# The cosine attention of a two-layer megakernel, written out straight in batches of six tiles instead of a loop over heads in batches of four

## Chip, core and metric

One core of one Trainium2 chip. The metric is device time in microseconds (us) of one launch, median of several runs.

## What is computed

X is (2, 2048, 256) in float32. Each of two layers forms `x + attention(LN(x)) * silu(ffn(LN(x)))` with 16 heads of 16 columns. Layer 0 has an inverse-distance attention and stays as it was. Layer 1, which the change rewrites:

```
Q, K = l2norm(heads(x Wq)), l2norm(heads(x Wk)); V = heads(x Wv)
cos = clip(Q K^T, -0.999, 0.999)
W = (1 - arccos(cos) / pi) ** 16;  W = W / (sum(W) + 1e-6)
out = (W V) Wo + bo
ffn = relu(x Wq1^T + b1) Wq2^T + b2        (Wq1, Wq2 ternary)
```

## The kernel before

`program` runs phases one after the other, each a block of five engine programs: weights, norm, projection, attention, output, for each layer. `attention_phase` serves both layers by `if L == 0`.

A **unit** is 128 keys of one head and one batch entry against all 2048 queries: 128 x 2048 float32, 32 units a head, 512 in layer 1. For each unit of layer 1: TensorE forms the scores in two PSUM halves `psS` (L751); VectorE clips each half into a slot of `ring` (L1054) and multiplies it with itself from PSUM into `q_ring` (L1063); ScalarE takes Ln(1 - cos^2) (L1011) and Sigmoid of -0.5 times that (L1016); VectorE multiplies with the cosine, the tangent of half the angle ("tangents", L1094); ScalarE takes Arctan (L1021). The 16th power is then split by columns: ScalarE does 1312 of 2048 by Ln and Exp (L1027, L1033), VectorE 224 by one affine instruction and four squarings (L1074, L1078), GpSimd (POOL) 512 in the same way (L712, L716). TensorE then adds the weighted values into `psO` (L774).

The work goes in **batches** of `BATCH = 4` units, eight a head; `ring` has eight slots (two batches) and `q_ring` four. ScalarE's instructions take two units at a time except Sigmoid (one). A `powers` call on VectorE or POOL handles a batch as two halves, each one affine and four squarings, taken alternately, so ten instructions. ScalarE changes its table set twice a batch: before Sigmoid and before the second Ln.

Order on each engine for batch j: VectorE: clip and square of batch j, powers of j-1, tangents of j. ScalarE: Ln, Sigmoid, Arctan, table load, Ln, Exp, of j. POOL: powers of j, after **both** Arctans of the batch (`pool.wait_ge(s_at, ...)`, L707). TensorE: scores one unit ahead, then the weighted values of j-1. In every fourth batch comes the work of a **tile** n (16 units, one head and batch entry): ScalarE copies the head's output (L820), TensorE transposes it (L782), VectorE divides it by its sum (`dve_out`, L838 to L855) into `gated` in SBUF, and 128 tokens of the FFN pass: hidden (L795, L801), Relu (L827), sum (L810), copy (L833), and a store issued from ScalarE (L835). Hidden stands in one piece behind the weighted values of its batch.

`pairs` (L668) gives TensorE, ScalarE, VectorE and SyncE the first head, a `Fori` loop over 14 heads, and the last head; POOL's program is straight. SyncE loads the stacks of the next tile (12 DMAs) and `ffn_in`. POOL copies each head's values into `v_tile` (L704). The output phase of layer 1 finds `gated` in SBUF and loads two arrays in four pieces each (`n_loads`, L1124); that of layer 0 loads three.

Of the kernel before, what the change touches and what calls it, by code (L numbers as in the profile page):

```python
# [52 lines left out]
class Mem:  # L53


    def __init__(self, nc, ctx):
# [351 lines left out]
def projection_phase(nc, m, io, L):  # L408
# [23 lines left out]
    with ExitStack() as ctx:  # L432
# [6 lines left out]
        (s_xT,) = sems(nc, ctx, pre, "xT_stored")  # L439
# [3 lines left out]
        def _(sp):  # L443
# [21 lines left out]
            if L == 1:  # L465
                sp.wait_ge(s_xT, 16)
            if L == 0:
# [166 lines left out]
def attention_phase(nc, m, io, L):  # L634


    pre = f"a{L}"
# [3 lines left out]
    q_ring = m.area(RING * T, 4, T)  # L641
# [3 lines left out]
    ACT_POW, DVE_POW = 1312, 1536  # L645
    POW_STEPS = 10
    BATCH = 4
    ACT_SQ = 384
    rows = ROWS + NORM_ROWS if L == 0 else ROWS
    loads = 2 * len(PRODUCTS) + (2 if L == 0 else 0)  # L650
    values = m.values[:, :, :].rearrange("p (b k) (h d) -> p b k h d", b=B, h=HEADS)
    gated = m.gated[:, :, :].rearrange("p (b q a) (h d) -> p b q a h d", b=B, q=QB, h=HEADS)
    EPS_SUM = SHEP_EPS if L == 0 else SUM_EPS1
    with ExitStack() as ctx:
# [3 lines left out]
        if L == 0:  # L658
            s_a, s_y, s_m, s_v, s_wa, s_wd, s_r2, s_g0 = sems(
                nc, ctx, pre, "inv_dist", "quot", "guarded", "inv_shifted", "w_act", "w_dve", "ffn_squared", "gated0")  # L660
        else:
            s_cl, s_q, s_rs, s_ls, s_z, s_at, s_ln, s_w, s_pw, s_pp = sems(
                nc, ctx, pre, "clipped", "cos2", "rsin", "log_sin", "tan_half", "angle", "log", "w_act", "w_dve",
                "w_pool")
# [11 lines left out]
        def _(sp):  # L676
            def head(h, first, last):
                for b in range(B):
# [4 lines left out]
                    for side, stack in ((0, m.q_stack[b]), (1, m.k_stack[b])):  # L683
# [4 lines left out]
                        if L == 0:  # L688
                            at = ROWS + 3 * side
                            sp.dma_start(stack[at:at + 3, :],  # L690
                                         io["norm_parts"][:, bass.ds(h + HEADS * side, 1), tok]
                                         .rearrange("a o t -> (a o) t")).then_inc(s_stk[b], 16)
# [7 lines left out]
        def _(pool):  # L700
            def value_tile(h, b, first):
                if not first:
# [3 lines left out]
            def powers(h, j):  # L706
                pool.wait_ge(s_at, UNITS // 2 * h + 2 * j + 2)  # L707
                at = (BATCH * j) % RING
                parts = [ring[:, at + 2 * i:at + 2 * i + 2, DVE_POW:T] for i in range(2)]
                done = POW_STEPS * (UNITS // BATCH * h + j)  # L710
                for part in parts:
                    nc.gpsimd.tensor_scalar(part, part, 2.0 / PI, 0.5, ALU.mult, ALU.add).then_inc(s_pp, 1)  # L712
                for i in range(2, POW_STEPS):
                    part = parts[i % 2]
                    pool.wait_ge(s_pp, done + i - 1)
                    nc.gpsimd.tensor_tensor(part, part, part, ALU.mult).then_inc(s_pp, 1)  # L716

            def guard(c):
                pool.wait_ge(s_y, 2 * c + 2)
                if c + 1 >= LAG_SQ:  # L720
                    pool.wait_ge(s_wd, c + 2 - LAG_SQ)
# [3 lines left out]
            def head(h, first, last):  # L725
                if L == 0:
                    for u in range(UNITS):
                        if u % KT == 3:
                            value_tile(h, u // KT, first)
                        guard(UNITS * h + u)  # L730
                else:
                    for j in range(UNITS // BATCH):
                        if j == 0:
                            value_tile(h, 0, first)
                        if j == 2:
                            value_tile(h, 1, first)
                        powers(h, j)
            for h in range(HEADS):
                head(h, h == 0, h == HEADS - 1)

        def pe_scores(pe, h, u, first, halves=(0, 1)):
# [3 lines left out]
            for half in halves:  # L745
                if not (first and u == 0):

                    pe.wait_ge(s_y if L == 0 else s_q, 2 * (UNITS * h + u) + half - 1)
# [7 lines left out]
        def pe_values(pe, h, u, first):  # L756
# [8 lines left out]
            if L == 0:  # L765
                pe.wait_ge(s_wa, n + 1)
                pe.wait_ge(s_wd, n + 1)
            else:
                pe.wait_ge(s_w, n + 1)
                pe.wait_ge(s_pw, POW_STEPS * (UNITS // BATCH * h + u // BATCH + 1))  # L770
                pe.wait_ge(s_pp, POW_STEPS * (UNITS // BATCH * h + u // BATCH + 1))

# [13 lines left out]
        def pe_hidden(pe, n, quarters=range(4)):  # L786

            for quarter in quarters:
# [3 lines left out]
                for f in range(2 * (quarter % 2), 2 * (quarter % 2) + 2):  # L792
                    for k in range(KD):
                        c = (4 * g + f) * P
                        last = nc.tensor.matmul(m.psM[g][:, f * P:(f + 1) * P], m.w1T[:, k, c:c + P],  # L795
                                                m.ffn_in[:, k, :], start=k == 0 and (L == 0 or f == 0),
                                                stop=L == 0 and k == KD - 1)
                if quarter % 2 == 0:
                    continue
                if L == 1:  # L800
                    last = nc.tensor.matmul(m.psM[g][:, :], m.b1_tiles[:, :],  # L801
                                            m.ident[0:FT, 4 * g:4 * g + 4].unsqueeze(2).broadcast_to([FT, 4, P]),
                                            start=False, stop=True)
                last.then_inc(s_h, 1)

        def pe_ffn_sum(pe, n, fs=range(FT)):
            if fs[0] == 0:
                pe.wait_ge(s_r if L == 1 else s_r2, 2 * (n + 1))
            for f in fs:
                last = nc.tensor.matmul(m.psM[0][:, 0:D], m.hidden[:, f, :], m.w2T[:, f, :], start=f == 0,  # L810
                                        stop=L == 0 and f == FT - 1)
            if L == 1:
                last = nc.tensor.matmul(m.psM[0][:, 0:D], m.ones_row[0:1, :], m.b2_row[0:1, :], start=False, stop=True)
# [24 lines left out]
        def dve_out(dve, h, b, n):  # L838
# [5 lines left out]
            nc.vector.tensor_scalar(den, ps[:, :, :, DH], EPS_SUM, None, ALU.add).then_inc(s_den, 1)  # L844
# [5 lines left out]
            if L == 0:  # L850
                nc.vector.tensor_tensor(out, ps[:, :, :, 0:DH], out, ALU.mult).then_inc(s_g0, 1)
                dve.wait_ge(s_g0, n + 1)
                nc.vector.tensor_tensor(out, out, rec16, ALU.mult).then_inc(s_g, 1)
            else:
                nc.vector.tensor_tensor(out, ps[:, :, :, 0:DH], rec16, ALU.mult).then_inc(s_g, 1)  # L855

        if L == 0:

            OUT_COPY, OUT_T, OUT_DIV = 5, 7, 8
            HID = (0, 1, 2, 3)  # L860
            RELU, SQ = (2, 4), (4, 6)
            SUM = {8: (0,), 9: (1,), 10: (2,), 11: (3,), 12: (4,), 13: (5,), 14: (6, 7)}
            COPY = 15

            @block.tensor
            def _(pe):
                def head(h, first, last):
                    for u in range(UNITS + (LAG_PV if last else 0)):
                        b, kt = u // KT, u % KT
                        n = 2 * h + b  # L870
# [408 lines left out]
```

## Time and profile before

| | us |
|---|---|
| median of 3 runs | 7410.69 (7410.47 to 7413.83) |
| the profiled execution | 7411.12 |
| its span in the trace | 7409.3 |
| layer 1, first to last start of a batch's tangents | 2843.81 to 7290.03 |

Busy time of each engine over the span: VectorE 6974.3, ScalarE 6691.4, TensorE 4119.9, POOL 3180.5. Read a row as: start, length, engine, line, operation, output<-input, shape, count; in brackets the idle time before it and what ended it.

### The profile page before, as it was taken

What the parts mean: (1) busy time and instruction counts of PE and PEld (TensorE: products, weight loads), DVE (VectorE), ACT (ScalarE), POOL (GpSimd) and SP (SyncE); (2) the same over time, 40 slices, a digit from 0 to 9 for tenths busy, and PEclk for the clock granted to TensorE, in tenths of its full rate; (3) what the DMA queues carried; (4) which work ended last, traced back from release to release, by engine and by line L of the source; (5) the groups of instructions that cost most, each with busy time, mean ns of one, the idle gap of its engine ahead of it and who ended that gap; (6) DMA issues with size and microseconds to landing.
All of it is one profiled execution on the core that took longest, in us unless ns stands there. A gap on an engine that the chain in (4) does not pass through costs nothing. (4 is left out here: it accounts for less than half of the span.)

```text
span 7409.3 us, 61195 instructions
## 1 busy us (share of the span) xinstructions
PE 4119.9 (56%) x17232; PEld 1274.3 (17%) x17232; DVE 6974.3 (94%) x6415; ACT 6691.4 (90%) x4385; POOL 3180.5 (43%) x1860
## 2 busy tenths in 40 slices
PE   6666666676666774444445444444444444444445
PEld 3222222222222331111111111111111111111112
DVE  7899999999999768999999999999999999999996
ACT  3799999999999647999999999999999999999995
POOL 0244444444444203544554454454445445544542
PEclk8888888888888886556566656656666666666657
DMA  3100000000000221000000000000000000000002
GB/s 129 46 18 17 12 17 12 17 17 12 17 14 15 100 84 32 7 6 11 7 6 11 7 6 11 7 6 11 7 6 7 10 6 7 11 6 7 11 2 70
DMA packets 113682, 148.47 MB, mean 20 GB/s; under 512 B 17038, under 2 KB 98857, under 8 KB 112634
## 3 DMA queue, kind: packets, MB, share of 16 engines
q1 hardware_dynamic: 104314, 138.54, 6.1%
q10 hardware_dynamic: 9216, 8.39, 0.3%
q14 instruction: 116, 0.95, 0.0%
q8 instruction: 36, 0.59, 0.0%
HBM read 91.55 MB, written 55.31 MB: 20 GB/s over the span
## 5 line engine op out<-in xcount | busy, mean ns | idle before, releaser
L751 PE MATMUL psS<-q_stack,k_stack 102*128 102x512 bf16 (+1 forms) x4096 | 1756.3, 523 | 2397.0 <-DVE work L1063 1619.6
L716 POOL TENSOR_TENSOR work<-work 128x1024 f32<-128x1024 f32 x1024 | 1915.9, 1907 | 10.2
L774 PE MATMUL psO<-work,v_tile 128*32 128x512 f32 x8192 | 1378.6, 794 | 729.8 <-DVE work L1078 722.8
L723 POOL TENSOR_SCALAR work<-work 128x2048 f32<-128x2048 f32 x512 | 970.5, 1896 | 1527.0 <-DVE work L955 1274.8
L1054 DVE TENSOR_SCALAR work<-psS 128x1024 f32<-128x1024 f32 x1024 | 1207.3, 1220 | 74.9 <-issue 41.0
L943 DVE SCALAR_TENSOR_TENSOR work<-work,psS 128x1024 f32<-128x1024 f32 x1024 | 1216.1, 1216 | 51.3 <-ACT work L901 50.2
L712 POOL TENSOR_SCALAR work<-work 128x1024 f32<-128x1024 f32 x256 | 267.5, 1045 | 2305.1 <-ACT work L1021 2294.9
L1063 DVE TENSOR_TENSOR work<-psS,work 128x1024 f32<-128x1024 f32 x1024 | 1201.5, 1216 | 0.0
L1094 DVE SCALAR_TENSOR_TENSOR work<-work 128x2048 f32<-128x2048 f32 x512 | 1138.9, 2287 | 62.3 <-ACT work L1016 60.5
L901 ACT ACTIVATE work<-psS 128x1024 f32<-128x1024 f32 x1024 | 1062.2, 1038 | 119.0 <-PE psS L751 86.0
L1011 ACT ACTIVATE work<-work 128x4096 f32<-128x4096 f32 x256 | 922.7, 3612 | 130.4 <-DVE work L1063 120.4
L916 ACT ACTIVATE work<-work 128x2048 f32<-128x2048 f32 x512 | 986.4, 1927 | 2.6 <-POOL work L723 2.2
L955 DVE TENSOR_TENSOR work<-work 128x1664 f32<-128x1664 f32 x512 | 970.1, 1895 | 0.2 <-ACT work L916 0.2
L751 PEld LDWEIGHTS psS<-q_stack,k_stack 102*128 102x128 bf16 (+1 forms) x4096 | 269.6, 106 | 3995.6 <-DVE work L1063 2520.0
L1016 ACT ACTIVATE work<-work 128x2048 f32<-128x2048 f32 x512 | 935.9, 1898 | 1.4
L1021 ACT ACTIVATE work<-work 128x4096 f32<-128x4096 f32 x256 | 924.1, 3610 | 6.9
L1027 ACT ACTIVATE work<-work 128x2624 f32<-128x2624 f32 x256 | 597.9, 2383 | 1.4
L1033 ACT ACTIVATE work<-work 128x2624 f32<-128x2624 f32 x256 | 595.7, 2374 | 0.0
L1078 DVE TENSOR_TENSOR work<-work 128x448 f32<-128x448 f32 x1024 | 572.4, 629 | 0.0
L774 PEld LDWEIGHTS psO<-work,v_tile 128*32 128x32 f32 x8192 | 250.3, 135 | 1560.7 <-issue 808.3
L1074 DVE TENSOR_SCALAR work<-work 128x448 f32<-128x448 f32 x256 | 293.7, 1187 | 3.8 <-ACT work L1021 3.8
L795 PEld LDWEIGHTS psM<-ffn_in,w1T 128*128 128x128 f32 x2048 | 270.9, 202 | 75.3 <-issue 57.9
(126 smaller groups left out, 3186.7 us busy)
## 6 DMA issues: line engine op xcount, KB each, us to landing
qk_parts<-work SPq DMA_DIRECT2D x64, 384.0 KB, 3.2
q_stack<-qk_parts SPq DMA_DIRECT2D x384, 64.0 KB, 2.2
k_stack<-qk_parts SPq DMA_DIRECT2D x384, 64.0 KB, 2.2
ffn_in<-xT_store SPq DMA_DIRECT2D x64, 128.0 KB, 2.5
y_store<-ffn_out ACTq DMA_DIRECT2D x64, 128.0 KB, 1.7
work<-y_store SPq DMA_DIRECT2D x8, 1024.0 KB, 12.0
work<-in_x SPq DMA_DIRECT2D x1, 4096.0 KB, 14.4
xn_store<-work SPq DMA_DIRECT2D x1, 4096.0 KB, 13.0
```

Of the source, the lines that this page charges most:

```text
L716: nc.gpsimd.tensor_tensor(part, part, part, ALU.mult).then_inc(s_pp, 1)
L723: nc.gpsimd.tensor_scalar(slot, slot, F32_MAX, 0.0, ALU.min, ALU.max).then_inc(s_m, 1)
L751: last = nc.tensor.matmul(m.psS[half][:, q * 512:(q + 1) * 512], m.k_stack[b][0:rows, kt * P:(kt + 1) * P], m.q_stack[b][0:rows, c:c + 512 ...
L774: last = nc.tensor.matmul(m.psO[b][VW * q:VW * (q + 1), :], m.v_tile[b][:, kt, :], ring[:, u % RING, q * 512:(q + 1) * 512], start=kt == 0 ...
L901: nc.scalar.activation(ring[:, u % RING, half * 1024:(half + 1) * 1024], m.psS[half][:, :], ACT.Abs_reciprocal_sqrt, bias=ZERO_SHIFT)\
L916: nc.scalar.activation(slot, slot, ACT.Abs_reciprocal_sqrt, bias=SHEP_EPS * SHEP_EPS, scale=2 * SHEP_EPS).then_inc(s_v, 1)
L943: nc.vector.scalar_tensor_tensor(part, part, 0.5 / SHEP_EPS, m.psS[half][:, :], ALU.add, ALU.mult).then_inc(s_y, 1)
L955: nc.vector.tensor_tensor(part, part, part, ALU.mult).then_inc(s_wd, 1)
L1016: nc.scalar.activation(slot, slot, ACT.Sigmoid, scale=-0.5).then_inc(s_rs, 1)
L1054: nc.vector.tensor_scalar(ring[:, u % RING, half * 1024:(half + 1) * 1024], m.psS[half][:, :], COS_MAX, -COS_MAX, ALU.min, ALU.max)\
L1063: nc.vector.tensor_tensor(q_ring[:, u % BATCH, cols], m.psS[half][:, :], ring[:, u % RING, cols], ALU.mult).then_inc(s_q, 1)
L1094: nc.vector.scalar_tensor_tensor(slot, q_ring[:, u % BATCH, :], RSIN_MAX, slot, ALU.min, ALU.mult).then_inc(s_z, 1)
```

## The change

Layer 0's attention becomes `distance_phase`, instruction for instruction as before. Layer 1's becomes `cosine_phase`:

- no loop on any engine: 86 batches written out, sizes 4, 84 times 6, 4;
- one region of 18 slots: two batches of cosines (12) and one of squares (6). `values` and `gated` lie in it, so the projection phase stores the values to DRAM (`v_store`), SyncE loads each tile's values from there straight into `v_tile` (rows of 64 bytes), and each head's output goes from a small staging buffer to `o_store`, also by SyncE; the output phase loads it back (three loads a piece) and its transposes wait for that;
- first Ln in instructions of 3, 2 and 1 units, Sigmoid of 1, 1, 2, 2, Arctan, the later Ln and Exp of 3 and 3;
- column split 1328 / 192 / 528 (ScalarE / VectorE / POOL) instead of 1312 / 224 / 512;
- POOL's and VectorE's affine of the first half waits for the first Arctan alone; TensorE's weighted values of the first half wait for the first half's powers;
- order on VectorE: tangents of i, head's output, clip and square of i+1, powers of i (cyclically as before);
- FFN hidden in four pieces, one behind the scores of each of four units; Relu and the copy between the first Ln and Sigmoid; the store of the FFN from SyncE;
- the table load at the head of each loop turn goes.

```diff
-        self.values = sb("values", [P, NT, D])
-        self.gated = sb("gated", [P, NT, D])
-        self.work = sb("work", [P, 3 * NT * D])
+        self.work = sb("work", [P, 5 * NT * D])
+        self.values = self.area(3 * NT * D, NT, D)
+        self.gated = self.area(4 * NT * D, NT, D)
...
+                if L == 1:
+                    sp.wait_ge(s_vfree, 4 * i + 6)
+                    sp.dma_start(io["v_store"][:, bass.ds(4 * i, 4), :], m.values[:, bass.ds(4 * i, 4), :])\
+                        .then_inc(s_vst, 16)
...
+def cosine_phase(nc, m, io):
+    BATCH = 6
+    LANES = 18
+    sizes = [4] + [BATCH] * ((TOTAL - 8) // BATCH) + [4]
+    ACT_POW, DVE_POW = 1328, 1520
...
+        @block.sync
...
+            for n in range(TILES):
+                if n >= B:
+                    sp.wait_ge(s_qk, 2 * KT * (n - 1))
...
+                if n >= B:
+                    sp.wait_ge(s_pv, KT * (n - 1))
+                sp.dma_start(m.v_tile[b][:, :, 0:DH], v_view[:, b, :, h, :]).then_inc(s_vt[b], 16)
+                if n > 0:
+                    sp.wait_ge(s_h, 2 * n)
+                sp.dma_start(m.ffn_in[:, :, :], io["xT_store"][:, :, n * P:(n + 1) * P]).then_inc(s_fin, 16)
+                if n >= 2:
+                    stores(n - 2)
...
+        @block.tensor
...
+            for i in range(NB + 2):
...
+                for at in range(max(len(ahead), 4)):
+                    if at < len(ahead):
+                        scores(ahead[at])
+                    if at < 4:
+                        for n in tiles:
+                            ffn_hidden(n, at)
+                if 1 <= i <= NB:
+                    for g in range(starts[i - 1], starts[i]):
+                        weighted(g)
...
+        @block.scalar
...
+                    for p, size in log_parts(i):
+                        act.wait_ge(s_q, 2 * (starts[i] + p + size))
+                        nc.scalar.activation(square(p, size), square(p, size), ACT.Ln, bias=1.0, scale=-1.0)\
+                            .then_inc(s_ls, size)
+                    ffn_part(i)
+                    act.wait_ge(s_ls, starts[i + 1])
+                    for p, size in tan_parts(i):
...
+                    for p, size in thirds(i):
+                        act.wait_ge(s_z, starts[i] + p + size)
+                        nc.scalar.activation(cosine(i, p, size), cosine(i, p, size), ACT.Arctan).then_inc(s_at, 1)
...
+        @block.vector
...
+            for i in range(NB + 2):
+                if i < NB:
+                    tangents(i)
+                for n in range(TILES):
+                    if last_batch[n] + 2 == i:
+                        head_out(n)
+                if i + 1 < NB:
+                    for g in range(starts[i + 1], starts[i + 2]):
+                        clip_and_square(g)
+                if i < NB:
+                    powers(i)
...
+        @block.gpsimd
+        def _(pool):
+            for j in range(NB):
+                parts = [cosine(j, p, size)[:, :, DVE_POW:T] for p, size in thirds(j)]
+                for c, part in enumerate(parts):
+                    pool.wait_ge(s_at, 2 * j + c + 1)
...
-        n_loads = 3 if L == 0 else 2
+        n_loads = 3
```

## Rows read from the trace of the kernel before

**Rows 1.** The page, busy time of each engine over the span

```profile
PE 4119.9 (56%) x17232; PEld 1274.3 (17%) x17232; DVE 6974.3 (94%) x6415; ACT 6691.4 (90%) x4385; POOL 3180.5 (43%) x1860
```

**Rows 2.** Timeline of VectorE: a head's output, then one whole batch of layer 1

```profile
4006.31 0.17 DVE L844 TENSOR_SCALAR den<-psM 128x16 f32<-128x16 f32 x1
...
4007.28 2.35 DVE L1054 TENSOR_SCALAR work<-psS 128x1024 f32<-128x1024 f32 x2
...
4067.32 8.90 DVE L1094 SCALAR_TENSOR_TENSOR work<-work 128x2048 f32<-128x2048 f32 x4 [0.26 <-ACT work L1016]
4076.36 2.35 DVE L1054 TENSOR_SCALAR work<-psS 128x1024 f32<-128x1024 f32 x2
...
4094.74 2.71 DVE L1074 TENSOR_SCALAR work<-work 128x448 f32<-128x448 f32 x2
4097.37 4.36 DVE L1078 TENSOR_TENSOR work<-work 128x448 f32<-128x448 f32 x8
4101.73 8.90 DVE L1094 SCALAR_TENSOR_TENSOR work<-work 128x2048 f32<-128x2048 f32 x4
```

**Rows 3.** Timeline of POOL in the same batch; the third row from a narrower window

```profile
4079.95 2.17 POOL L712 TENSOR_SCALAR work<-work 128x1024 f32<-128x1024 f32 x2 [17.43 <-ACT work L1021]
4082.20 15.00 POOL L716 TENSOR_TENSOR work<-work 128x1024 f32<-128x1024 f32 x8
...
4095.16 2.04 POOL L716 TENSOR_TENSOR work<-work 128x1024 f32<-128x1024 f32 x1
```

**Rows 4.** Timeline of ScalarE in the same batch, and a Relu pair

```profile
4055.64 1.06 ACT L827 ACTIVATE hidden<-psM 128x512 f32<-128x512 f32 x2
...
4072.59 7.27 ACT L1021 ACTIVATE work<-work 128x4096 f32<-128x4096 f32 x2
4079.88 1.28 ACT L1022 ACT_TABLE_LOAD   x1
4081.18 4.67 ACT L1027 ACTIVATE work<-work 128x2624 f32<-128x2624 f32 x2
...
4090.32 0.36 ACT L833 ACTIVATE ffn_out<-psM 128x256 f32<-128x256 f32 x1
...
4091.30 7.18 ACT L1011 ACTIVATE work<-work 128x4096 f32<-128x4096 f32 x2 [0.62 <-ACT ffn_out L833]
```

**Rows 5.** Timeline of VectorE: second and fifth batch of the first head; a loop turn

```profile
2843.81 8.90 DVE L1094 SCALAR_TENSOR_TENSOR work<-work 128x2048 f32<-128x2048 f32 x4 [6.90 <-ACT work L1016]
...
2947.01 8.90 DVE L1094 SCALAR_TENSOR_TENSOR work<-work 128x2048 f32<-128x2048 f32 x4
...
3937.41 2.36 DVE L1054 TENSOR_SCALAR work<-psS 128x1024 f32<-128x1024 f32 x2 [3.10 <-issue]
```

**Rows 6.** Groups by line and shape, 3000 to 7000 us: busy us, mean ns

```profile
L1016 ACT ACTIVATE work<-work 128x2048 f32<-128x2048 f32 x456 | 833.6, 1898 | 1.3
L1016 ACT ACT_TABLE_LOAD x114 | 146.3, 1283 | 2.1
```

**Rows 7.** The page's groups: POOL's affine of layer 0 on 2048 columns

```profile
L723 POOL TENSOR_SCALAR work<-work 128x2048 f32<-128x2048 f32 x512 | 970.5, 1896 | 1527.0 <-DVE work L955 1274.8
```

**Rows 8.** Timeline of VectorE, the last batch of layer 1

```profile
7290.03 8.90 DVE L1094 SCALAR_TENSOR_TENSOR work<-work 128x2048 f32<-128x2048 f32 x4
...
7305.02 17.93 DVE L1078 TENSOR_TENSOR work<-work 128x448 f32<-128x448 f32 x8
```

**Rows 9.** Timeline of ScalarE, the first Silu of layer 0's and layer 1's output

```profile
2535.34 1.91 ACT L1186 ACTIVATE work<-work 128x2048 f32<-128x2048 f32 x1 [11.89 <-DMA work<-in_x]
...
7343.76 1.91 ACT L1186 ACTIVATE work<-work 128x2048 f32<-128x2048 f32 x1 [8.44 <-DMA work<-x_store]
```

**Rows 10.** The page, DMA issues: KB each, median us to landing

```profile
y_store<-ffn_out ACTq DMA_DIRECT2D x64, 128.0 KB, 1.7
```

**Rows 11.** Timeline of TensorE, weighted values of one batch

```profile
4032.10 5.89 PE L774 MATMUL psO<-work,v_tile 128*32 128x512 f32 x32 [5.27 <-DVE work L1078]
```

**Rows 12.** Stretches: busy us of PE, PEld, DVE, ACT, POOL; granted clock; scores, then FFN hidden

```profile
4010.80:4027.00 16.20, 8.28 (x16) 1.05 (x16) 16.20 (x14) 14.29 (x7) 16.04 (x11) 0.50 0.00 0
...
4037.90:4044.10 6.20, 6.16 (x40) 4.31 (x36) 5.71 (x4) 6.14 (x3) 0.00 (x0) 1.00 0.01 1
```

More of the change, by code:

```diff
@@ L466, in _ @@
                 sp.wait_ge(s_xT, 16)
+                sp.wait_ge(s_vst, 16 * TB)
             if L == 0:
@@ L700, in _, with value_tile @@
         def _(pool):
-            def value_tile(h, b, first):
-                if not first:
+            def value_tile(h, b):
+                if h > 0:
                     pool.wait_ge(s_pv, UNITS * h + KT * b + KT - UNITS)
                 nc.gpsimd.tensor_copy(m.v_tile[b][:, :, 0:DH], values[:, b, :, h, :]).then_inc(s_vt, 1)
[L706 to L716, printed above, removed]
             def guard(c):
@@ new lines, in dve_out, with _, head @@
+            nc.vector.tensor_tensor(out, ps[:, :, :, 0:DH], out, ALU.mult).then_inc(s_g0, 1)
+            dve.wait_ge(s_g0, n + 1)
+            nc.vector.tensor_tensor(out, out, rec16, ALU.mult).then_inc(s_g, 1)
+        OUT_COPY, OUT_T, OUT_DIV = 5, 7, 8
+        HID = (0, 1, 2, 3)
+        RELU, SQ = (2, 4), (4, 6)
+        SUM = {8: (0,), 9: (1,), 10: (2,), 11: (3,), 12: (4,), 13: (5,), 14: (6, 7)}
+        COPY = 15
+        @block.tensor
+        def _(pe):
+            def head(h, first, last):
+                for u in range(UNITS + (LAG_PV if last else 0)):
+                    b, kt = u // KT, u % KT
+                    n = 2 * h + b
+                    if u < UNITS:
+                        pe_scores(pe, h, u, first, (0,))
+                    if not (first and u < LAG_PV):
+                        pe_values(pe, h, u - LAG_PV, first)
+                    if u < UNITS:
+                        pe_scores(pe, h, u, first, (1,))
+                    if kt == 0 and not first:
+                        pe.wait_ge(s_g, n - 1)
+                    if kt == 2 and not (first and b == 0):
+                        pe.wait_ge(s_yo, n)
+                    if kt in HID and u < UNITS:
+                        pe_hidden(pe, n, (HID.index(kt),))
+                    if kt == OUT_T and u < UNITS and not (first and b == 0):
+                        pe.wait_ge(s_r, 2 * n + 1)
+                        pe_out(pe, n - 1)
+                    if kt in SUM:
+                        pe_ffn_sum(pe, n, SUM[kt])
+                if last:
+                    pe_out(pe, 2 * HEADS - 1)
+            pairs(pe, head)
@@ new lines, in _, with head, quotient @@
+        @block.vector
+        def _(dve):
+            def head(h, first, last):
+                def quotient(u, half):
+                    c = UNITS * h + u
+                    dve.wait_ge(s_a, 2 * c + half + 1)
+                    part = ring[:, u % RING, half * 1024:(half + 1) * 1024]
+                    nc.vector.scalar_tensor_tensor(part, part, 0.5 / SHEP_EPS, m.psS[half][:, :],
+                                                   ALU.add, ALU.mult).then_inc(s_y, 1)
+                for u in range(UNITS + (LAG_SQ if last else 0)):
+                    b, kt = u // KT, u % KT
+                    n = 2 * h + b
+                    c = UNITS * h + u
+                    if u < UNITS:
+                        quotient(u, 0)
+                    if not (first and u < LAG_SQ):
+                        dve.wait_ge(s_v, c - LAG_SQ + 1)
+                        part = ring[:, (u - LAG_SQ) % RING, ACT_SQ:T]
+                        nc.vector.tensor_tensor(part, part, part, ALU.mult).then_inc(s_wd, 1)
+                    if u < UNITS:
+                        quotient(u, 1)
+                    if kt == OUT_DIV and not (first and b == 0) and u < UNITS:
+                        dve_out(dve, h if b else h - 1, 1 - b, n - 1)
+                    if kt in SQ:
+                        g = HALVES[SQ.index(kt)]
+                        dve.wait_ge(s_r, 2 * n + SQ.index(kt) + 1)
+                        part = m.hidden[:, 4 * g:4 * g + 4, :]
+                        nc.vector.tensor_tensor(part, part, part, ALU.mult).then_inc(s_r2, 1)
+                if last:
+                    dve_out(dve, HEADS - 1, 1, 2 * HEADS - 1)
+            pairs(dve, head)
```

575 lines of the change are left out of this document (292 added, 283 removed).

## The prediction

> **What bounds the kernel now.** I read the page first, then the groups by line of the middle of layer 1, then the timelines of VectorE, POOL and ScalarE over two batches, and the waits last. The page [rows 1] shows VectorE busy for 94% and ScalarE for 90%; either could be called the bound, and neither figure says what sets a batch's length. The timelines do. Layer 1 repeats one batch 128 times; from the start of one batch's tangents to the next is 4101.73 - 4067.32 = 34.41 us [rows 2]. Inside it a chain goes round through three engines:
>
> - four tangents on VectorE, 8.90 [rows 2];
> - the second Arctan, which waits for the fourth tangent: 3.62, since 4072.59 + 7.27 = 4079.86 and the tangents end at 4076.22 [rows 2, 4];
> - POOL's ten instructions, from 4079.95 to 4097.20: 17.25, and 0.09 ahead of them [rows 3];
> - the rest of VectorE's second affine, 0.17, and its eight squarings, 4.36 [rows 2].
>
> The sum, 8.90 + 3.64 + 0.09 + 17.25 + 0.17 + 4.36 = 34.41, is the whole period. VectorE looks full because it is: it clips and squares until 4094.74, but then its two affines take 2.71 us where they need some 0.6, and end only when POOL does. The first waits for a POOL squaring that ends near 4095.2, the second for the next, which ends at 4097.20 and itself took 2.04 us [rows 2, 3]. So POOL is on the path with 43% busy.
>
> From the first tangents to the last are 7290.03 - 2843.81 = 4446.2 us [rows 5, 8], over 127 periods 35.01 each. Straight batches run at (2947.01 - 2843.81) / 3 = 34.40 [rows 5]; a loop turn adds a 3.10 us stop in which VectorE waits for nothing the profile shows [rows 5], about 0.37 a batch. The remaining 0.24 goes with the tiles' FFN and output work.
>
> **The change: the period of six.** Each term is scaled from a row.
>
> Tangents: four in 8.90, the last 2.29, so steps of 2.20; six take 5 x 2.20 + 2.29 = 13.3. The second Arctan: 2048 columns take 1.90 [rows 6], 4096 take 3.62, so 0.84 ns a column and 5.34 for 6144. POOL: its affine takes 1.04 on 1024 columns (a pair is 2.17) and 1.90 on 2048 [rows 7], hence 1.51 on 3 x 528 = 1584; the first half's now runs early, so one is on the path. Its squaring steps are (15.00 - 2.04) / 7 = 1.85. The trace has one size of it: in proportion to columns it would be 2.86; with a fixed part of 0.19, as the affine has, 2.76. I take 2.80, between close bounds: 22.4 for eight. With starts, POOL costs 0.09 + 1.51 + 0.08 + 22.4 = 24.1. VectorE's affines: from 0.2, if one slips in before POOL's last squaring, to 0.75, if both must follow it. Relative to the end of the tangents, clip and square takes 6 x 4.6 (18.38 for four, 4076.36 to 4094.74), so VectorE arrives at 27.7 and POOL ends at 5.3 + 24.1 = 29.4: less than one squaring is left, nearer to both following. I take 0.6. Squarings: 0.54 a step for 448 columns against 2.20 for 2048 of the tangents, about 1.03 ns a column, so 0.68 for 576, and 5.4 for eight. **Chain: 13.3 + 5.4 + 24.1 + 0.6 + 5.4 = 48.8 us for six units**, 8.13 a unit against 8.60.
>
> The skill bears on this sharing. The Trainium skill's SBUF — State Buffer, section "SBUF: two separate sides", says that the pair which VectorE and GpSimd share is an exclusive lock held for the full instruction; the rows agree (2.08 us for a 448-column affine next to POOL's 2.04). It speaks against this change in that each hold grows from 1.9 to 2.8 us. By that rule both affines follow POOL, 0.75, and the time is 13 us above my sum; with no lock they take 0.2, 34 us below it.
>
> ScalarE must fit too. Neighbours overlap by about 0.1, so steps are 1.80, 3.57 and 5.29 for one, two and three units; for 3 x 1328 columns, the pair of 2624 takes 4.67, of which one is 1.90 + 576 x 0.84 ns = 2.38, so a step of 2.29, and 2.29 + 1360 x 0.84 ns = 3.43. First Ln 5.29 + 3.57 + 1.90 = 10.8; Sigmoid 2 x 1.80 + 3.57 + 3.61 = 10.8; Arctan 10.6; second Ln and Exp 4 x 3.43 = 13.7; two table loads 2 x 1.29 = 2.6 [rows 4, 6]. That is 48.5. A tile adds Relu 0.96, the FFN copy 0.27 (it is 0.98 to the next instruction now, with the DMA issued behind it [rows 4]; the issue goes to SyncE) and the head's copy about 0.5, half the Relu pair on the same 512 columns: 1.7 per 16 units, 0.65 per six. **ScalarE: 49.1 on average**, now the longer by a hair. Table loads fall from 2 x 128 + 16 to 173; 99 x 1.28 = 127 us of ScalarE. The Trainium skill's ScalarE: Activation LUTs, section "What happens when an `exp` ACTIVATE runs", prices a load at about 2.7 us with its drain, by which that saving would be 267 us; the trace has 1.28 and it decides.
>
> Both chains meet in each batch, so I add what the four-unit kernel loses beside the loop: 0.3. Another 0.3 stands for TensorE's pieces. The scores take 2.07 us a unit at a granted clock of 0.50 (1.2 GHz) beside 4.6 of VectorE [rows 12]; all of hidden took 6.2 us at 1.00 (2.4 GHz), a piece about 1.0 to 2.1, twice that at the lower clock. An odd piece may hold the scores by 0 to 2 us, twice a tile; with the head's output (0.97, 4006.31 to 4007.28 [rows 2]) that exceeds the 1.7 us for which VectorE would have waited for POOL anyway by about 0.8 a tile. The weighted values, 6 x 1.47 = 8.8 us [rows 11], end before the 13.3 of tangents do. **Period: 49.1 + 0.6 = 49.7 us.**
>
> **What costs nothing, and its cover.** The loop turns, 14 x 3.1 us, are in the 35.01 and not in the 49.7. SyncE's queue is in order: 12 stack loads, the wait for the weighted values two tiles back, `v_tile`, the wait for hidden, `ffn_in`, then the stores of two tiles back. All these waits are passed at three batches behind the previous tile's last, 2.3 batches (115 us) before the next stacks are needed. ScalarE's FFN copy waits for the store before it, issued a batch (50 us) earlier, against 1.7 to land [rows 10]; 64-byte rows may make it ten times that and are still covered. If that cover went, ScalarE would stop, and scores with it. POOL's copies of the values go from where it waits for ScalarE.
>
> **The ends.** First period: tangents 8.9, clip and square of six units 27.6 (POOL is done before that), then the last Ln, table load and first Sigmoid 1.9 + 1.3 + 1.9: 41.7. The last six-unit period has a four-unit batch behind it: -3.5. After the last tangents the chain is as before; VectorE and POOL take their squarings in turn there, 17.93 us for eight against 4.36 [rows 2, 8]. The last head's store must land before the block ends: 1.7 [rows 10] for as many bytes in long rows, ten times that at most; I take 5. The output phase waits for a third load: 11.89 against 8.44 in layer 0, where there are three [rows 9]: +3.5. The last value store: 0 to 3, I take 0.5.
>
> **Sum.** 41.7 + 84 x 49.7 - 3.5 = 4213.0 instead of 4446.2: -233.2. With +9.0, 7411.12 - 224.2 = 7186.9. The profiled execution lies 0.4 above the median, so I predict **7187**.
>
> **Rivals.**
> *POOL's early start collides (12%).* The first half's affine may start while the last tangents run and hold one for up to 1.5 us, which delays the second Arctan, and with it all. For: both read SBUF twice or in pairs. Against: if ScalarE is never idle, the first Arctan ends 16.0 after the first Sigmoid's start, when the sixth tangent is ending. 84 x 1.5: 7313.
> *Hidden in pieces holds the scores (12%).* All at the lower clock, 4 us late a tile plus 0.95, less 1.7 of cover: 3.3 x 32 = 104 us in place of the 25 I allow: 7266.
> *Straight code starves an engine (5%), and the kernel is slower.* The place: the instruction stream of VectorE or ScalarE, 86 batches long. If each batch brought a stop like the one at a loop turn, 3.1 us [rows 5], it would be 7187 + 84 x 3.1 = 7447; from 224 / 84 = 2.7 us a batch on, all is lost. Against: the first head is straight and holds 34.40 without a stop [rows 5].
> *The batch size gives nothing (3%).* If periods scaled as units (34.64 x 1.5 = 52.0), 7380 would come, by the loop turns alone.
>
> **How the numbers follow.** Forecast 66%, the rivals 32%, the last 2% several together. The forecast's own bounds: POOL squarings of 2.76 to 2.86 are -0.3 to +0.5 a period, affines -0.4 to +0.15, the pieces -0.3 to +0.5; period 48.7 to 50.9, so 7103 to 7288. The range goes on over the first two rivals: 7110 to 7330. This kernel can be told from no change from about 0.2% (15 us) on. Faster by more: all but the straight-code rival and a few mishaps, 0.92; within, 0.02; slower, 0.06.
>
> **What would show it.** Right: 84 starts of tangents 49 to 50.5 us apart; POOL's eight squarings in 22.1 to 22.9; VectorE's affines ending just behind them; no stop marked issue; the first Silu idle near 12. Wrong: tangents of more than 2.3 us with POOL busy, scores late in batches with hidden, a store that ScalarE waits for, or periods over 52.

## The result and the profile after

The changed kernel takes 7169.31 us (7163.55 to 7177.40, 4 executions) against 7410.60: ratio 0.9674 (0.9657 to 0.9691), 241 us less. Forecast were 7187 and a range of 7110 to 7330. The profiled execution is the longest of the four, 7177.40 with a span of 7175.6. It is 7177.40 - 7411.12 = -233.7 us against the profiled execution of before, and this difference is what the accounts below explain. The batches hold six units, not six tiles as the title has it: a tile is 16 units.

Page of the kernel after, busy time of each engine, as in [rows 1]:

```profile
PE 4122.8 (57%) x17232; PEld 1407.8 (20%) x17232; DVE 6747.7 (94%) x5995; ACT 6510.5 (91%) x3866; POOL 3153.3 (44%) x1408
```

VectorE and ScalarE lost 227 and 181 us of work, yet their shares stand where they stood. Again only a timeline tells what sets a batch's length. VectorE after, as in [rows 2, 5]: the first batch's tangents, then one plain batch, that is one without work of the FFN.

```profile
2847.74 4.49 DVE L1184 SCALAR_TENSOR_TENSOR work<-work 128x2048 f32<-128x2048 f32 x2 [5.20 <-ACT work L1144]
...
4072.79 2.22 DVE L1192 TENSOR_SCALAR work<-work 128x576 f32<-128x576 f32 x2
4074.94 5.41 DVE L1195 TENSOR_TENSOR work<-work 128x576 f32<-128x576 f32 x8
4080.28 13.29 DVE L1184 SCALAR_TENSOR_TENSOR work<-work 128x2048 f32<-128x2048 f32 x6
...
4123.71 5.42 DVE L1195 TENSOR_TENSOR work<-work 128x576 f32<-128x576 f32 x8
```

POOL and ScalarE in the same batch, as in [rows 3, 4]:

```profile
4093.36 1.58 POOL L1232 TENSOR_SCALAR work<-work 128x1584 f32<-128x1584 f32 x1 [19.22 <-ACT work L1148]
4099.00 1.51 POOL L1232 TENSOR_SCALAR work<-work 128x1584 f32<-128x1584 f32 x1 [4.07 <-ACT work L1148]
4100.60 22.32 POOL L1235 TENSOR_TENSOR work<-work 128x1584 f32<-128x1584 f32 x8
```

```profile
4087.96 5.31 ACT L1148 ACTIVATE work<-work 128x6144 f32<-128x6144 f32 x1
4093.60 5.32 ACT L1148 ACTIVATE work<-work 128x6144 f32<-128x6144 f32 x1 [0.33 <-DVE work L1184]
```

From squarings to squarings is 4123.71 - 4074.94 = 48.77, and it is one chain without a gap: squarings 5.34, tangents 13.32, second Arctan 5.32, start 0.08, POOL's affine 1.60, POOL's squarings 22.32, and 0.79 until VectorE's affines are through. I forecast 48.8 for it. ScalarE waits 0.33 us in this batch, ahead of its second Arctan. The first affine of POOL starts 0.21 us before the sixth tangent ends and takes 1.58 instead of 1.51; no tangent is longer for it.

Of the 84 six-unit periods, the 22 without FFN work take 48.77. The 31 with the pieces of hidden run from 48.3 to 51.0 and average 49.68; the 31 after them, with the sum and ScalarE's copy, average 49.6. The mean is 49.41, against 49.7 forecast.

| stretch, us | before | forecast | after |
|---|---|---|---|
| start of the trace to the first tangents | 2843.8 | +0.5 | 2847.7 (+3.9) |
| first to last tangents | 4446.2 | 4213.0 | 4196.8 (-249.4) |
| of it the first period | 34.3 | 41.7 | 46.1 (2893.82 - 2847.74) |
| last tangents to the end of attention | 41.0 | 0 | 37.8 (-3.2) |
| end of attention to the end | 78.3 | +8.5 | 93.2 (+14.9) |

**Where the pieces of hidden cost.** TensorE, then VectorE, then a stretch of the kernel after (busy us of PE, PEld, DVE, ACT, POOL; then the granted clock):

```profile
4153.51 1.92 PE L1071 MATMUL psM<-ffn_in,w1T 128*128 128x128 f32 x8
4155.36 2.07 PE L1074 MATMUL psM<-ident,b_tiles 8*128 8x512 f32 x2
```

```profile
4158.50 2.36 DVE L1173 TENSOR_SCALAR work<-psS 128x1024 f32<-128x1024 f32 x2 [1.19 <-PE psS L1029]
```

```profile
4150.00:4156.00 6.00, 5.09 (x17) 3.15 (x17) 5.93 (x6) 6.00 (x3) 6.00 (x3) 0.50 0.00 0
```

At 0.50, that is 1.2 GHz, the second piece with its bias takes 3.9 us, and VectorE then waits about 1.19 us for scores. The fourth piece does the same where the clock is at 0.50. In other batches one or both of them take 2.1 to 3.0 us, the shorter of these at 2.4 GHz, and no wait follows. The lengths sort by it: the nine periods with both waits take 50.7 to 51.0 us, the thirteen with one 49.3 to 49.7, the eight with none 48.9 to 49.2 (the last period, before a batch of four, stands apart with 48.3).

These periods do not explain why executions differ by 14 us. The changed kernel, `pool_late`, `act_less`, `sig_single` and `warm_output` run the same instructions up to the first tangents of layer 1, and in their traces this stretch takes from 2841.3 to 2859.3 us. From first to last tangents the changed kernel and `warm_output`, again the same instructions, differ by 4.6 us only. Beside the experiments the kernel before spread by 7 to 15 us too.

**The output phase** after: the first Silu, as in [rows 9].

```profile
7103.03 1.91 ACT L1324 ACTIVATE work<-work 128x2048 f32<-128x2048 f32 x1 [12.62 <-DMA work<-x_store]
```

The first load is issued 6.7 us after attention's last work on VectorE, where it was 2.9 before: the head's store costs 3.7. The third load costs 4.2 (14.0 from the first load, at 7089.04, to Silu against 9.8). The remaining 7.0 were not foreseen. The phase goes through the tokens in pairs of 128-token blocks, each with its transposes and matmuls on TensorE. TensorE begins after 21.7 us of idling; its granted clock is 0.50 from 7103 to 7122, and the first three pairs take 7.5, 6.6 and 6.3 us, where later pairs take 3.4.

That is how this execution went, not what the change costs. In the traces of `pool_late`, `act_less`, `batch4`, `sig_single`, `batch4_fit`, `batch4_logs` and `old_split` TensorE idles 20.0 to 21.4 us at the same place, yet only the first pair is slow, and from the end of attention to the end are 85.6 to 86.6 us; in `log_halves` it is 87.3, in `ffn_block` 89.3. Against 78.3 before, most of them are 7.3 to 8.3 us longer, for a forecast of 8.5.

### The profile page after: what moved, and what is told of

It is laid out like the page before. It is cut to its first block and busy times, and to the rows that moved or that the text cites. A ratio compares the mean times of both kernels' runs of the same rounds, so it can differ in the third digit from the quotient of the medians.

```text
span 7175.6 us, 55838 instructions
## 1 busy us (share of the span) xinstructions
PE 4122.8 (57%) x17232; PEld 1407.8 (20%) x17232; DVE 6747.7 (94%) x5995; ACT 6510.5 (91%) x3866; POOL 3153.3 (44%) x1408
## 5 line engine op out<-in xcount | busy, mean ns | idle before, releaser
L1029 PE MATMUL psS<-q_stack,k_stack 96*128 96x512 bf16 x2048 | 1014.6, 600 | 1675.9 <-DVE work L1178 1615.0
L1235 POOL TENSOR_TENSOR work<-work 128x1584 f32<-128x1584 f32 (+1 forms) x688 | 1908.4, 2810 | 6.9
L1232 POOL TENSOR_SCALAR work<-work 128x1584 f32<-128x1584 f32 (+1 forms) x172 | 261.6, 1521 | 2387.0 <-ACT work L1148 2387.0
L1184 DVE SCALAR_TENSOR_TENSOR work<-work 128x2048 f32<-128x2048 f32 x512 | 1139.6, 2282 | 34.3 <-ACT work L1144 33.7
L723 PE MATMUL psS<-q_stack,k_stack 102*128 102x512 bf16 x2048 | 719.3, 438 | 712.1 <-DVE work L900 675.9
L873 ACT ACTIVATE work<-work 128x2048 f32<-128x2048 f32 x512 | 987.5, 1929 | 2.6 <-POOL work L705 2.2
L1139 ACT ACTIVATE work<-work 128x4096 f32<-128x4096 f32 (+2 forms) x258 | 909.0, 3577 | 53.9 <-DVE work L1178 53.9
L1148 ACT ACTIVATE work<-work 128x6144 f32<-128x6144 f32 (+1 forms) x172 | 907.3, 5275 | 26.5 <-DVE work L1184 26.5
L1144 ACT ACTIVATE work<-work 128x2048 f32<-128x2048 f32 (+1 forms) x342 | 915.7, 2748 | 1.0
L1153 ACT ACTIVATE work<-work 128x3984 f32<-128x3984 f32 (+1 forms) x172 | 592.3, 3490 | 1.0
L1157 ACT ACTIVATE work<-work 128x3984 f32<-128x3984 f32 (+1 forms) x172 | 590.8, 3482 | 0.0
L1195 DVE TENSOR_TENSOR work<-work 128x576 f32<-128x576 f32 (+1 forms) x688 | 480.9, 766 | 0.0
```

The costliest lines, as they stand in the source:

```text
L873: nc.scalar.activation(slot, slot, ACT.Abs_reciprocal_sqrt, bias=SHEP_EPS * SHEP_EPS, scale=2 * SHEP_EPS).then_inc(s_v, 1)
L1029: last = nc.tensor.matmul(m.psS[half][:, q * 512:(q + 1) * 512], m.k_stack[b][0:ROWS, kt * P:(kt + 1) * P], m.q_stack[b][0:ROWS, c:c + 512 ...
L1139: nc.scalar.activation(square(p, size), square(p, size), ACT.Ln, bias=1.0, scale=-1.0)\
L1144: nc.scalar.activation(square(p, size), square(p, size), ACT.Sigmoid, scale=-0.5)\
L1184: nc.vector.scalar_tensor_tensor(cosine(j, p), square(p), RSIN_MAX, cosine(j, p), ALU.min, ALU.mult).then_inc(s_z, 1)
L1235: nc.gpsimd.tensor_tensor(parts[i % 2], parts[i % 2], parts[i % 2], ALU.mult).then_inc(s_pp, 1)
```

## The experiments

My theory: the chain through POOL sets the period. Twelve kernels ran, in three groups, each on a chip of its own with the kernel before beside it. That took 7416.6 us beside the first four, 7412.9 beside `ffn_block`, `sig_single`, `batch4_fit` and `warm_output`, and 7415.3 beside the others; each ratio is against the time of its group. Across groups a difference of a few us between medians says nothing, and the periods of the traces are the finer measure. The first four runs ask what bounds six and what the batch size is worth.

### POOL a little later

```diff
+                pool.wait_ge(s_at, 2 * j + 2)
                 for c, part in enumerate(parts):
-                    pool.wait_ge(s_at, 2 * j + c + 1)
```

> The changed kernel, but POOL's first affine waits for both Arctans, as before the change. Chain theory: POOL's work behind the second Arctan grows by 1.51 + 0.08 = 1.6 us a batch, the plain period from 48.77 to 50.4, less where ScalarE's FFN work already made room (about a third of it): 84 x 1.2 to 1.6, so 7270 to 7304. Rival, ScalarE's sum is the bound: 7169 to 7185.

Measured: 7241.9, ratio 0.9763 (0.9747 to 0.9780), 73 us over the changed kernel, and 28 us below my range. A plain period is 50.04 to 50.05, +1.27 and not +1.6. The rows show where 0.45 came back: POOL's eight squarings, then VectorE's affines in the next batch.

```profile
4070.47 22.44 POOL L1235 TENSOR_TENSOR work<-work 128x1584 f32<-128x1584 f32 x8
```

```profile
4089.84 3.48 DVE L1192 TENSOR_SCALAR work<-work 128x576 f32<-128x576 f32 x2
```

VectorE arrives at 4089.84, more than one POOL squaring ahead of POOL's end at 4092.91, so one affine slips in between two squarings. VectorE's own squarings start at 4093.25, 0.34 behind POOL's end, where it was 0.79. POOL's start is on the path: the sum of ScalarE does not bound a plain batch.

### ScalarE lighter (part of the power left out)

```diff
-                        part = cosine(i, p, size)[:, :, 0:ACT_POW]
+                        part = cosine(i, p, size)[:, :, 0:ACT_POW - 128]
```

> The changed kernel, but ScalarE's second Ln and Exp leave out 128 of their 1328 columns, which then get no power: part of the computation is left out. ScalarE is lighter by 4 x 3 x 128 x 0.84 ns = 1.3 us a batch. Chain theory: plain periods stay at 48.7 to 48.8 and only those made longer by FFN work on ScalarE shrink, by 0.6 on average: 7169 - 84 x 0.4 = 7135 give or take 12. Rival, ScalarE's sum is the bound: 7169 - 84 x 1.3 = 7060.

Measured: 7162.0, ratio 0.9653 (0.9637 to 0.9669); not told apart from the changed kernel, and 15 us above my range. Plain periods stay at 48.77 exactly, which rules the rival out. But the others hardly shrank either: the mean is 49.38 against 49.41, for ScalarE's 1.3 us less. POOL and ScalarE of this run:

```profile
4099.74 2.50 POOL L1232 TENSOR_SCALAR work<-work 128x1584 f32<-128x1584 f32 x1 [18.29 <-ACT work L1148]
```

```profile
4100.91 5.32 ACT L1148 ACTIVATE work<-work 128x6144 f32<-128x6144 f32 x1 [1.25 <-DVE work L1184]
```

With ScalarE early, the first Arctan ends before the tangents do and the second waits 1.25 us for them: the time that ScalarE is given comes back as that wait. POOL's first affine now starts during the last tangent and takes 2.50 instead of 1.51. That is the meeting that the first rival spoke of, but it is POOL that waits: the six tangents beside this row take 13.29 us, as ever, and none of the run's 512 is longer than 2.3. The affine has time to spare, so the meeting costs the period nothing.

### The kernel before without its loop

```diff
-            with eng.Fori(1, HEADS - 1) as h:
-                body(h, False, False)
+            if L == 0:
+                with eng.Fori(1, HEADS - 1) as h:
+                    body(h, False, False)
+            else:
+                for h in range(1, HEADS - 1):
+                    body(h, False, False)
```

> The kernel before with layer 1's 14 loop turns written out, nothing else. If a turn costs the 3.1 us stop of VectorE and little more: 7411 - 14 x 3.0 = 7369, and one table load a head stays. Rival, the loop carries most of the gain: under 7300. Rival, straight code starves an engine: over 7411.

Measured: 7385.8, ratio 0.9955 (0.9938 to 0.9972), some 31 us less than the 7416.6 beside it, for 42 expected. The stop marked issue, ahead of the first clip of a loop turn, is gone from VectorE's waits. The loop accounts for about an eighth of the change's gain, and straight code starves nothing here.

### Batches of four in the new code

```diff
-    BATCH = 6
-    LANES = 18
+    BATCH = 4
+    LANES = 12
```

> The changed kernel with BATCH = 4 and 12 slots: straight code, new column split, pieces of hidden, early affine all stay; 128 batches of four. Chain theory (tangents, second Arctan, POOL, squarings go round): 8.9 + 3.7 + POOL 0.1 + 1.1 + 0.1 + 8 x 1.90 = 16.5, + 0.5 + 8 x 0.48 = 3.8, so 33.4 a batch; ScalarE with its share of FFN needs 33.9; with friction 34.2. 127 x 34.2 against 4196 measured from first to last tangents: about 7317. Rival, the loop's removal is what paid and the batch size little: below 7220.

Measured: 7508.9, ratio 1.0122 (1.0105 to 1.0139): slower than the kernel before. My theory missed by 190 us. Most batches with hidden take 39.15 against 34.5 to 34.9 for the rest. ScalarE in one of them:

```profile
4059.48 0.60 ACT L1117 ACTIVATE hidden<-psM 128x512 f32<-128x512 f32 x1 [2.41 <-PE psM L1074]
```

With only four units the fourth piece stands behind the last scores, so Relu waits for it, and table load, Sigmoid and tangents wait behind Relu; the tangents of this batch start 4.40 us late. Six units hide what four expose. The experiment did not isolate the batch size; the runs `ffn_block`, `batch4_fit` and `batch4_logs` take its faults out.

### Hidden in one piece again

```diff
-                    if at < 4:
-                        for n in tiles:
-                            ffn_hidden(n, at)
...
+                for n in tiles:
+                    for quarter in range(4):
+                        ffn_hidden(n, quarter)
```

It stands behind the weighted values; Relu and copy go behind Exp, the sum to the next batch.

> The changed kernel with the FFN placed as before the change: hidden in one piece behind the weighted values, Relu and copy behind Exp, the sum a batch later. Theory: the pieces run at 1.2 GHz, each second one with its bias holds the scores 1.2 us, and 31 periods with hidden average 49.68 with a spread up to 51.0; in one piece behind the weighted values nothing waits, so the long ones go: 10 x 1.4 + some of the rest, 7145 to 7160. Rival, the pieces cost nothing as POOL covers them: 7165 to 7175. Rival, one piece behind the weighted values reaches into the next scores: over 7180.

Measured: **7147.6** (7145.67 to 7156.98), ratio 0.9645 (0.9631 to 0.9658), inside my range: 22 us less than the changed kernel's median. The executions have no time in common, though the intervals of the two ratios just touch, and the traces bear the difference out below. TensorE of this run:

```profile
4025.91 2.05 PE L1071 MATMUL psM<-ffn_in,w1T 128*128 128x128 f32 x16
```

Sixteen in 2.05 us where eight took 1.92: right behind the weighted values the clock has risen to 1.00. All of hidden takes 6.1 us here, and VectorE's waits for scores are gone: 0.8 us from 2860 to 7040, against 40.9 in the changed kernel. Periods with hidden average 48.9, those with the head's output 49.3, the longest of all is 49.70, and the mean falls from 49.41 to 49.15. From first to last tangents that is 25.5 us less; the tail of the last batch gives 5 back, since FFN work now stands behind it. The edit moved hidden, Relu, the copy and the sum together; of these, hidden in four pieces is what the waits for scores hang on. The FFN's new place is the part of the change that costs.

### Six single Sigmoids

```diff
-        return [(0, 1), (1, 1), (2, 2), (4, 2)] if sizes[j] == 6 else [(0, 1), (1, 1), (2, 2)]
+        return [(p, 1) for p in range(sizes[j])]
```

> The changed kernel with six one-unit Sigmoids instead of 1, 1, 2, 2. Theory: after a period with hidden the tangents start right behind the first Sigmoid and then wait 0.81 us for the two-unit one; this makes periods of 49.68 of 31 that would be near 49.0. ScalarE pays 2 x 0.05 us. So 7169 - 31 x 0.6 = 7150, give or take 6. Rival, those periods are long because ScalarE's FFN work is in them (Relu 0.96, copy 0.27): unchanged or a few us more, 7169 to 7178.

Measured: 7157.9 (7150.45 to 7167.13), ratio 0.9658 (0.9645 to 0.9671). The mean period falls from 49.41 to 49.28, 11 us, but the executions overlap the changed kernel's: a small gain where I expected 19 us, and not settled.

### Batches of four, fitted

`ffn_block` with single Sigmoids, four units to a batch, and the first Ln in 2 and 2:

```diff
-    BATCH = 6
-    LANES = 18
+    BATCH = 4
+    LANES = 12
...
-        return [(0, 3), (3, 2), (5, 1)] if sizes[j] == 6 else [(0, 2), (2, 1), (3, 1)]
+        return [(0, 2), (2, 2)]
...
-        return [(0, 1), (1, 1), (2, 2), (4, 2)] if sizes[j] == 6 else [(0, 1), (1, 1), (2, 2)]
+        return [(p, 1) for p in range(sizes[j])]
```

> The run ffn_block with six one-unit Sigmoids and BATCH = 4 (first Ln in 2 and 2). Isolates the batch size. Chain theory: 33.4 to 33.9 plain, 34.2 on average, 127 periods: 7300 to 7325, about 150 above ffn_block. Rival, the other parts of the change carry most of the gain and the size little: under 7250.

Measured: 7386.1, ratio 0.9965 (0.9952 to 0.9978), plain periods 34.57: where the kernel before without its loop stands (0.9955, plain periods 34.52), though POOL's path is 0.8 us shorter. My chain fell here. ScalarE and VectorE of this run:

```profile
4018.79 3.62 ACT L1139 ACTIVATE work<-work 128x4096 f32<-128x4096 f32 x1 [1.82 <-DVE work L1176]
```

```profile
4025.66 8.89 DVE L1182 SCALAR_TENSOR_TENSOR work<-work 128x2048 f32<-128x2048 f32 x4 [2.11 <-ACT work L1143]
```

The second Ln waits for the last clip and square, and the tangents for Sigmoid. A second chain goes round and leaves POOL out: clip and square, last Ln, table load, first Sigmoid, tangents. For four units it is 18.55 + 3.66 + 1.29 + 1.95 + 8.93 = 34.4, and with some 0.2 ahead of the Ln it is the 34.57.

### The logarithm in smaller and in larger parts

`batch4_logs` is `batch4_fit` with its first Ln in 2, 1, 1, as the changed kernel has it for its batch of four:

```diff
-        return [(0, 2), (2, 2)]
+        return [(0, 2), (2, 1), (3, 1)]
```

`log_halves` is `ffn_block` (six units) with the first Ln in halves of 3 and 3:

```diff
-        return [(0, 3), (3, 2), (5, 1)] if sizes[j] == 6 else [(0, 2), (2, 1), (3, 1)]
+        return thirds(j)
```

> The run batch4_fit with the first Ln in 2, 1, 1 units instead of 2, 2. Theory after batch4_fit: beside the chain through POOL a second one goes round, clip and square of the batch, its last Ln, table load, first Sigmoid, tangents: 18.55 + 3.66 + 1.29 + 1.95 + 8.93 = 34.4 with a two-unit Ln at the end, as measured; with one unit 32.7, under POOL's 33.3 and ScalarE's 33.9. So 34.0 on average, 7386 - 127 x 0.75 = 7290, between 7275 and 7310. That leaves some 145 us for the step from four to six. Rival, POOL's chain was the bound at four too: 7380 to 7390.

> The run ffn_block (batches of six) with the first Ln in 3 and 3 instead of 3, 2, 1. Second chain at six: 27.6 + 5.36 + 1.29 + 1.95 + 13.4, plus 0.8 where the tangents wait for the two-unit Sigmoid: 49.6 to 50.4, and 1 more where a head's output stands before clip and square. Mean 50.0 to 50.8 against 49.15: 7148 + 75 to 140 = 7223 to 7288. Rival, POOL's chain alone bounds six: 7143 to 7153.

Measured: `batch4_logs` 7293.1, ratio 0.9834 (0.9819 to 0.9849), mean period 34.01, inside my range. There ScalarE is busy for 2491.3 of the 2500 us from 4000 to 6500, so at four units with a one-unit last Ln its own sum is the bound, as the 33.9 of the expectation had it, and neither chain. `log_halves` 7335.6, ratio 0.9892 (0.9877 to 0.9907), plain periods 50.96. ScalarE and VectorE of `log_halves`:

```profile
4066.83 5.32 ACT L1139 ACTIVATE work<-work 128x6144 f32<-128x6144 f32 x1 [3.42 <-DVE work L1176]
```

```profile
4075.41 4.50 DVE L1182 SCALAR_TENSOR_TENSOR work<-work 128x2048 f32<-128x2048 f32 x2 [2.09 <-ACT work L1143]
```

Between its second and third tangent VectorE waits another 0.82 us for Sigmoid. The second chain closes: 27.9 clip and square, 0.2, 5.3, 1.3, 1.9, and 14.3 for tangents with their 0.82 pause, 50.9 together of 50.96. The size is 48 us above my upper end: clip and square takes 27.9 and not 27.6, and the pause comes in every batch. An estimate from these numbers: with the last Ln one unit long, 1.90 us instead of 5.32, this chain is some 3.4 us shorter, 47.6, and POOL's 48.77 bounds again, as measured. So the 3, 2, 1 is worth some 188 us in this kernel, and a one-unit last part some 93 us at four units.

### The old column split

On top of `ffn_block`:

```diff
-    ACT_POW, DVE_POW = 1328, 1520
+    ACT_POW, DVE_POW = 1312, 1536
```

> The run ffn_block with the column split of before, 1312 / 224 / 512. POOL: eight squarings 0.08 shorter each, -0.7; VectorE: eight squarings 0.1 longer each, +0.8; ScalarE -0.16. Chain theory: +0.1 a batch, ScalarE's share a bit less: 7140 to 7160. Rival, the split was worth much: over 7170.

Measured: 7158.8 (7155.15 to 7164.83), ratio 0.9653 (0.9640 to 0.9666), mean period 49.28 against 49.15 in `ffn_block`. Inside the range: by the periods the split is worth some 11 us, and the times alone do not tell the two kernels apart.

### TensorE kept busy ahead of the output

```diff
+                if L == 1 and n == 0:
+                    for _ in range(80):
+                        nc.tensor.transpose(m.psS[1][:, 0:P], m.ident[:, :], m.ident[:, :])
                 if L == 1 and n % CP == 0:
```

`ffn_warm` is the same on top of `ffn_block`.

> The changed kernel with 80 transposes into an unused PSUM buffer while the output phase waits for its loads. Theory: TensorE now begins that phase after 21.7 us of idling and runs its first pairs at the lower clock, 6.5 us each against 3.4; kept busy, it starts at 2.4 GHz and the phase is 8 to 12 us shorter: 7157 to 7161. Rival, the loads set those pairs' pace: unchanged.

> The run ffn_block together with the 80 transposes of warm_output. Both gains add: 7147.6 - 7 = 7141. Rival, the warm start is lost in what varies between executions or in the loads: 7145 to 7150.

Measured: 7167.3 (7155.48 to 7169.27) alone, 7148.4 (7144.20 to 7156.18) with `ffn_block`. Neither total can be told from its base, the first misses my 7157 to 7161, and the second lies where its rival had it. A stretch of `warm_output`, from its second pair on, then the same stretch of `act_less`, which has no dummy transposes:

```profile
7110.00:7120.00 10.00, 10.00 (x43) 6.48 (x42) 4.15 (x6) 3.59 (x4) 0.00 (x0) 1.00 1.09 377
```

```profile
7117.00:7127.00 10.00, 10.00 (x43) 6.48 (x42) 4.16 (x6) 3.59 (x4) 0.00 (x0) 1.00 1.08 367
```

In `warm_output` the phase from the end of attention takes 85.9 us, in `ffn_warm` 85.7, against 93.2 in the changed kernel's trace. Taken alone this looks like the mechanism at work. But the kernels without the transposes are as fast there (85.6 to 86.6 us in seven traces), and in `warm_output` the first pair still takes 6.5 us. So no gain of the transposes is shown; what they would cure is the late rise of the clock in two of the traces, the changed kernel's and `ffn_block`'s, and why it came late there stays open.

## Why the prediction was right, and where it was not

The sign, the range and the size held: 224 us forecast, 241 measured in the medians, 234 in the profiled executions. The closeness of the last is in part luck, for the misses partly cancel: the 84 periods came 20.6 us below their sum (49.41 each against 49.66), the first period 4.4 above, the ends 6.6 above.

- **Round chain of six, 48.8: right**, measured 48.77 and shown by `pool_late` and `act_less`. Its terms: tangents 13.3, POOL's squarings 22.4 (22.3 measured), VectorE's 5.4. The affines were under: 0.79 for my 0.6, both follow POOL.
- **ScalarE's sum as the base, 49.1, "now the longer by a hair": wrong.** The period was built as ScalarE's 49.1 plus 0.6, that is 0.9 over the chain; measured is 0.64 over it. ScalarE waits 0.33 us in a plain batch, and taking 1.3 us a batch from it moved the mean by 0.04 (`act_less`). The sum was nearly right as a number, but the chain bounds and ScalarE's sum does not.
- **"Both chains meet", +0.3, and TensorE's pieces, +0.3.** The lower clock and the hold of 1.2 us, once or twice in a tile, came as said; `ffn_block` takes 0.26 a period away. The 0.3 for the meeting was carried over from the kernel before, where it has another source (next point).
- **What bounds the kernel now: incomplete.** The sum of POOL's chain in [rows 2, 3, 4] is exact, but a second chain, clip and square to Ln to Sigmoid to tangents, stood within 0.2 us of it, and [rows 2] showed it, in the 0.26 us for which tangents waited for Sigmoid. Over 3000 to 7000 us of the kernel before that wait comes 57 times (total, times, longest):

```profile
DVE work L1094 <- ACT work L1016: 51.2, 57, 2.0
```

The 31 periods with a head's output, which stands ahead of clip and square, take 35.35 us there against 34.5 for plain ones, and 35.40 against 34.57 in `batch4_fit`, which the second chain bounds; in `batch4_logs`, where it is shorter, they take 33.65, no more than a plain one. So the 0.24 that I put down to the tiles' work is largely this chain. I used ScalarE only as a sum and the Ln split only as a length. By that text, batches of six with Ln in halves would have come out like the kernel with 3, 2, 1; they are 188 us apart. The forecast held because the change shortens both chains at once. The same omission made me expect 7300 to 7325 of `batch4_fit`, and the wait that made `batch4` slow, through Relu, table load and Sigmoid to the tangents, runs along this chain.
- **The loop**, 14 turns of 3.1 in my account: 43 us, of which `before_straight` gained 31.
- **First period, 41.7: missed by 4.4 us**: the tangents paused 0.81 for a two-unit Sigmoid, TensorE's pieces held the scores twice by 1.19, and the Relu pair, 1.07 us, stood between the last Ln and the table load.
- **Ends, +9: missed by 6.6** in the profiled execution. The store and load terms, 5 + 3.5, measured 3.7 + 4.2; the 5 was a guess between 1.7 and ten times that, and the store of 64-byte rows landed in 3.3 us. The last batch was 3.2 under. The 7.0 of TensorE at the lower clock and the 3.4 at the start are of this execution: other traces have the output phase 7 us shorter, and the start between 2841.3 and 2859.3.
- Rivals: POOL's early affine can meet the last tangent (`act_less`), and then POOL waits and no tangent does; pieces at the lower clock exist and cost a fifth of their price; straight code starves nothing (`before_straight`).
- On the lock that the prediction cites. The Trainium skill's SBUF — State Buffer, section "SBUF: two separate sides", has the first of VectorE and GpSimd to start hold the shared pair for its whole instruction, if VectorE's has two SBUF inputs or runs in a two-port mode. The traces agree with squarings of 2.8 us too: VectorE's two affines took 2.22 us and followed POOL's last squaring, in `pool_late` one went in between two squarings, and in `act_less` POOL's affine took 2.50 us behind a tangent that had started before it.

The gain as a ladder of ratios to the kernel before, each known to about 0.0015: loop away 0.9955 (`before_straight`); the other parts at four units and Ln in 2 and 2, 0.9965 (`batch4_fit`), so nothing more; last Ln one unit 0.9834 (`batch4_logs`); six units instead of four 0.9645 (`ffn_block`; its Sigmoids in 1, 1, 2, 2, where the rungs of four have them single); FFN in pieces 0.9674, the changed kernel. Lowest is `ffn_block`, 7147.6.

## What to carry to other kernels

Close the sum of one chain, then look for a second with a different engine left out: here a wait of a quarter microsecond on an otherwise full engine was its sign, and it is what a cure for the first chain will meet. Where one engine feeds a batched instruction on another piece by piece, look at the size of the **last** part: here it was on the path, while the parts of 3 and 2 ahead of it did not lengthen a plain batch. Work laid into gaps of an engine whose clock is low there can take twice as long as the same work next to a burst. And before a faster stretch in one trace is called an effect of an edit, look at the same stretch in other runs without the edit: here seven of them had the same 7 us without the dummy transposes.

## What was not expected of the hardware

TensorE's granted clock depended on what stood ahead of the work: hidden's 16 instructions took 2.05 us behind the weighted values and 3.8 between scores. It also differed between executions at the same place: after 20 to 22 us of idling the output phase began at 0.50 in every trace of the new code without the transposes, and rose after about one pair in seven of them and after nearly three in the changed kernel's. POOL's affine on 1584 columns took 2.50 us next to a tangent and 1.51 alone. VectorE's eight squarings in the last batch took 16.95 us beside POOL's, turn by turn as in [rows 8].
